# Row means of a two-layer convolution network on one core: taken from the rounded input and from sums kept in a first pass, instead of from the layer's output

## The reference

```python
def _L0_conv_ref(x, weight_int8, scale_weight, bias):
    scale_input = jnp.max(jnp.abs(x_cl)) / 2.0 ** (ACTBIT - 1)
    x_q = jnp.round(jnp.clip(x_cl / scale_input, -n, n))          # n = 127
    acc = conv3x3(x_q, w_hwio)                                    # padding 1
    out = acc * (scale_input * scale_weight) + bias
def _L1_conv_ref(x, w_real, w_imag, b_real, b_imag):
    X = jnp.fft.rfftn(x, axes=(-2, -1))
    Yr = _rconv(Xr, wr) - _rconv(Xi, wi) + b_real                 # 3x3 over frequencies
    Yi = _rconv(Xr, wi) + _rconv(Xi, wr) + b_imag
    return jnp.fft.irfftn(Y, axes=(-2, -1))

x = x + _L0_conv_ref(_gn(x), ...)
x = x + _L1_conv_ref(_gn(x), ...)
```

## Time and profile before

| | us |
|---|---|
| median of 3 runs | 3697.43 |
| lowest, highest | 3686.82, 3706.25 |
| profiled execution, its own time | 3688.6 |
| span of its trace | 3686.8 |
| mean granted TensorE clock, share of full | 0.995 |

### The profile page before, as it was taken

How to read it: one execution, slowest core, us unless ns; L and a number is a source line. 1 busy time by engine, 2 the same in 40 slices (tenths; PEclk the granted TensorE clock), 3 DMA queues, 4 the chain that set the end, 5 groups by cost and what they waited for, 6 DMA issues and landing times.

```text
span 3686.8 us, 126585 instructions
## 1 busy us (share of the span) xinstructions
PE 2952.2 (80%) x45732; PEld 2630.6 (71%) x45732; DVE 3147.2 (85%) x5880; ACT 1888.0 (51%) x2799; POOL 1481.3 (40%) x1984
## 2 busy tenths in 40 slices
PE   0000004899999999999999999999999999999998
PEld 0000002688888888888888888888888888888888
DVE  8999995688888888888888888888888888888886
ACT  8999991344444444444444444444444444444443
POOL 4777100344444444434443333443443433344444
PEclk9999999999999999999999999999999999999999
DMA  8777760366666666666666666666666666666655
GB/s 312 239 239 239 239 216 13 100 205 197 201 199 203 202 200 200 204 197 200 201 202 195 197 194 193 202 197 197 204 199 196 204 194 192 201 193 206 199 181 180
DMA packets 630696, 730.98 MB, mean 198 GB/s; under 512 B 76752, under 2 KB 602160, under 8 KB 614736
## 3 DMA queue, kind: packets, MB, share of 16 engines
q1 hardware_dynamic: 482640, 588.71, 50.1%
q10 hardware_dynamic: 147456, 134.28, 12.7%
HBM read 262.58 MB, written 134.22 MB: 108 GB/s over the span
## 4 chain that ended last, share of the span: by engine, by line
PE 54%; SPq 13%; DMA 11%; issue 11%; DVE 7%; ACTq 1%; ACT 1%; POOL 1%; DVEq 0%; POOLq 0%
PE y_ps L986 14%; PE mean_b L1031 9%; PE x_ps L973 7%; PE conv_ps L1018 7%; SPq L464 7%; PE fin_ps L1005 6%; DMA halo<-quant 4%; DMA out<-img 4%; PE t_ps L964 4%; SPq L386 3%; PE conv_ps L1020 2%; DVE scaled L763 2%; DMA img<-in_x 2%; PE fin_ps L1000 2%; DVE scaled L764 1%
## 5 line engine op out<-in xcount | busy, mean ns | idle before, releaser
L734 POOL TENSOR_SCALAR eo<-img,norm 128x256 f32<-128x256 f32 x512 | 477.9, 933 | 1458.5 <-PE t_ps L964 1248.9
L986 PEld LDWEIGHTS y_ps<-mix_w,stack 128*128 128x128 f16 x24576 | 793.5, 99 | 119.6 <-DMA stack<-xn 6.0
L986 PE MATMUL y_ps<-mix_w,stack 128*128 128x64 f16 x24576 | 809.3, 194 | 4.5 <-DMA stack<-xn 4.4
L562 ACT ACTIVATE y_hi<-y_ps 128x512 f16<-128x512 f32 x512 | 305.6, 597 | 889.3 <-PE y_ps L986 889.3
L548 ACT ACTIVATE xt<-t_ps 128x512 f32<-128x512 f32 x512 | 305.7, 597 | 629.2 <-PE t_ps L964 506.6
L973 PE MATMUL x_ps<-dft,xt 128*128 128x128 f32 x4096 | 541.6, 275 | 0.0
L839 DVE SCALAR_TENSOR_TENSOR img<-conv_ps,cst,img 128x512 f32<-128x512 f32 x512 | 383.1, 748 | 169.3 <-PE conv_ps L1020 153.1
L1031 PE MATMUL mean_b<-row_mean,img 128*128 128x48 f32 x4096 | 512.8, 273 | 8.4 <-DVE img L839 8.4
L1031 PEld LDWEIGHTS mean_b<-row_mean,img 128*128 128x128 f32 x4096 | 504.1, 196 | 18.2 <-DVE img L839 17.5
L826 DVE SCALAR_TENSOR_TENSOR xn<-x_ps,norm,xn 128x512 f16<-128x512 f32 x512 | 383.7, 750 | 140.7 <-ACT xn L555 120.0
L973 PEld LDWEIGHTS x_ps<-dft,xt 128*128 128x128 f32 x4096 | 498.3, 192 | 0.0
(11 more groups left out here) (134 smaller groups left out, 5111.6 us busy)
## 6 DMA issues: line engine op xcount, KB each, us to landing
stack<-xn SPq DMA_DIRECT2D x2048, 132.0 KB, 2.7
img<-in_x SPq DMA_DIRECT2D x1024, 128.0 KB, 2.9
out<-img ACTq DMA_DIRECT2D x1024, 128.0 KB, 3.0
img<-in_x SPq DMA_DIRECT2D x120, 1024.0 KB, 4.9
halo<-quant SPq DMA_DIRECT2D x192, 193.3 KB, 3.3
halo<-quant SPq DMA_DIRECT2D x64, 169.1 KB, 3.2
row_mean<-table_row_mean SPq DMA_DIRECT2D x1, 768.0 KB, 15.4
spread<-table_spread SPq DMA_DIRECT2D x1, 512.0 KB, 14.6
```

Source lines behind the costliest of these rows:

```text
L734: nc.gpsimd.tensor_scalar(even, rows[:, :, 0:F], norm[v][:, 2:3], None, ALU.add).then_inc(shift_s, 1)
L986: last = nc.tensor.matmul(y_ps[t % 2][:, g, b, :], stack[:, t % 2, g, first:first + F], mix_w[:, 2 * at + b, g, f, part, :], start=i == 0, ...
```

## The change

The row means of the result of layer 0 are no longer summed from that result. They are the sum of two parts. The first part are the row means of the input itself, and PE takes them in the first phase, while each image is there for its statistics; they are written to DRAM (`kept`, 128x96 float32 an image) and read back later. The second part are the row means of what layer 0 adds: the convolution commutes with the sum over rows, so the rounded input is summed over its rows first (`rounded_w`, 128 weights in float16: the three waves in two halves each, and the first and the last row) and a small product an image (`conv_a`) does the 3x3 weights after.

- First phase: PE gets `image_means`, 64 float32 products of 48 columns an image. They are of the form of the products that `row_means` did. PE waits for all tables before the first, and for ACT's copy of the image two before. SP waits for PE (`p1_pe`) too before it reloads a quarter, ACT waits for PE at the end of an image and copies the sums (`rmx`), SP stores them (`keep`).
- Main phase: `row_means` is now two float16 products of 258 columns a pair, right behind `conv_pair` of that pair, with its weights `rounded_w` and the moving `quant`. `mean_rows` at t = 12 is six small float32 products and the two that were there. ACT copies `rq_ps` at t = 9, DVE adds the two parts at t = 12 (`row_sum`), where ACT copied before. SP loads the kept sums at t = 6. DVE's rounding waits for `rq_s` (convolution and row means of the quarter) in place of `conv_s`.
- `quant`, `halo` and the layer 0 weights are float16 instead of bf16. Two tables of 768 KB and one of 1024 KB are loaded more, one of 768 KB less.

```diff
+    def image_means(i, u, tab):
+        n = 2 * i + u
+        for q in range(QU):
+            pe.wait_ge(load_s[u][q], loaded(i))
+            if q == 0:
+                pe.wait_ge(sums_s, n + 1)
+            for hb in range(QB * q, QB * q + QB):
+                for half in range(2):
+                    last = nc.tensor.matmul(sums_ps[u][half], img[u][:, hb, F * half:F * half + F], tab[:, 48 * hb:48 * hb + 48],
+                                            start=hb == 0, stop=hb == HB - 1)
+            last.then_inc(p1_pe, 1)
...
             pe.wait_ge(table_s, 16 * len(TABLES))
+            with pe.Fori(0, SP2 - 1) as i:
+                for u in range(2):
+                    image_means(i, u, sums[1])
+            for u in range(2):
+                image_means(SP2 - 1, u, sums[0])
...
+                        sp.wait_ge(p1_pe, (2 * i + u - 2) * QU + q + 1)
                         load_runs(2 * i + u + 2, u, q)
+                    keep(2 * i + u - 2, 2 * i + u, u)
...
+                act.wait_ge(p1_pe, QU * (n + 1))
+                act.wait_ge(kept_s[u], 16 * (i + 1))
+                nc.scalar.activation(rmx[:, u, 0:48], sums_ps[u][0], ACT.Copy)
+                nc.scalar.activation(rmx[:, u, 48:96], sums_ps[u][1], ACT.Copy).then_inc(sums_s, 1)
...
-            def row_means(k, u, c):
-                pe.wait_ge(x1_s, done(k, c))
-                if c == 0:
-                    pe.wait_ge(meanc_s, k + 1)
-                    nc.tensor.matmul(mean_b[:, 0:96], ident[:], zeros[:], start=True, stop=False)
-                for hb in (2 * c, 2 * c + 1):
-                    for half in range(2):
-                        nc.tensor.matmul(mean_ps[half], img[u][:, hb, F * half:F * half + F], row_mean[:, hb, :],
-                                         start=False, stop=False)
+            def row_means(k, c):
+                pe.wait_ge(quant_s, PAIRS * k + c + 1)
+                if c == 0:
+                    pe.wait_ge(rqe_s, k + 1)
+                for hb in (2 * c, 2 * c + 1):
+                    last = nc.tensor.matmul(rq_ps, rounded_w[:, hb, :], quant[:, hb, :], start=hb == 0, stop=hb == HB - 1)
+                last.then_inc(rq_s, 1)
+            def mean_rows(k, u):
+                pe.wait_ge(rqe_s, k + 2)
                 pe.wait_ge(zb_s, k + 1)
                 for half in range(2):
+                    for dw in range(3):
+                        nc.tensor.matmul(mean_ps[half], rq[:, F * half + dw:F * half + dw + F], conv_a[:, dw, :],
+                                         start=dw == 0, stop=False)
                     last = nc.tensor.matmul(mean_ps[half], norm[u][:, 2:3].to_broadcast([P, P]), channel[:],
...
-                    if conv and t == IMAGE_AT:
-                        act.wait_ge(mean_s, s + 2)
-                        nc.scalar.activation(row_t[:, 0, :], mean_ps[0], ACT.Copy)
-                        nc.scalar.activation(row_t[:, 1, :], mean_ps[1], ACT.Copy).then_inc(meanc_s, 1)
+                    if conv and t == STATS_AT - 1:
+                        act.wait_ge(rq_s, PAIRS * (s + 3))
+                        nc.scalar.activation(rq[:], rq_ps, ACT.Identity, scale=q_scale).then_inc(rqe_s, 1)
...
+            def row_sum(k, i, u):
+                dve.wait_ge(rmx_s[u], 16 * (i + 1))
+                dve.wait_ge(mean_s, k + 1)
+                nc.vector.tensor_tensor(row_t[:], misc_ps[:, 96:192].rearrange("p (a x) -> p a x", a=2),
+                                        rmx[:, u].rearrange("p (a x) -> p a x", a=2), ALU.add).then_inc(meanc_s, 1)
```

129 lines of the change are left out of this document (101 added, 28 removed).

## The result

| | before | after |
|---|---|---|
| median of 4 runs beside each other, us | 3694.26 | 3963.47 |
| lowest, highest | 3686.82, 3706.25 | 3939.27, 3968.39 |
| profiled execution, its own time | 3688.6 | 3959.38 |
| mean granted TensorE clock | 0.995 | 0.972 |

A forecast was written before the change was run, and what follows sets the result against it. The prediction took DVE's reductions to bound the first phase and PE the main phase. Its terms summed as 3688.6 + 299 - 15 - 186 = 3786.6, forecast 3787 us, 2.4% slower, range 3665 to 3880.

The forecast's parts named there:

- Part 1, the price of a product in the first phase: First phase: products stay at 1.2 GHz, 0.41 us each, 26.2 us an image, so PE becomes the bound: +299 us.
- Rival A: First phase: the clock rises, 13.4 us an image hides behind DVE, costing +15; total 3503 us; chance 0.17.
- Part 2, the ramp: First image's convolutions after the first phase: 12 steps get shorter without float32 means, -15 us, bounds -5 to -25.
- Part 3, a period of the main phase: Main phase: PE loses net 8.7 us of work an image; -6.0 a period taken, -186 us, bounds -78 to -295.
- Then what is late next: Main phase: halo waits grow, the statistics keep their latency, clock may fall; PE's 3.4 us idle a period set against it.
- the load at t = 6: Main phase: SP's 48 KB load is one issue in a queue with slack, costed at nothing.
- rival C: Main phase: PE falls to 1.2 GHz twice a period, gaining 2.6 us instead of 6.0; total 3892 us; chance 0.09.
- Rival B: Main phase: low clock holds in the first phase, but a period gains 9 us; total 3694, no change; chance 0.12.
- DVE as a floor: Main phase: DVE's 4.62 us lap is close behind PE's new 4.71 us step, so not all 8.7 us comes out.

The follow-up runs named there:

- E2: The kernel before with 64 float32 products an image added to its first phase and its old main phase kept: 4013.89 us, ratio 1.0884.
- E3: The changed kernel with the first phase's operands swapped: table columns as weights, 256 image columns moving, 32 products an image for 64: 3699.31 us, ratio 1.0025.
- E6: E1 with halo transfers for the first image only, later images reusing its rows: 3527.79 us, ratio 0.9523 to the kernel before.
- E5: E1 with the halo transfers issued ahead of `stack`'s in SP's queue, at the end of the step before: 3651.03 us, ratio 0.9847 to the kernel before.
- E10: The kernel before with E5's edit, halo transfers issued ahead of the restacking: 3699.84 us, ratio 1.0015.
- E4: E1 with SP loading the pair whose store was issued three steps ago instead of two: 3643.84 us, ratio 0.9868 to the kernel before.
- E9: E1 with image loads issued by GpSimd instead of SP, three steps behind their store: 3618.27 us, ratio 0.9785 to the kernel before.
- E8: E5 with the statistics' first product at t = 10 behind the convolution instead of in front: 3611.96 us, ratio 0.974 to the kernel before.
- E7: E1 with 16 unused float16 products ahead of the convolution at t = 1 and 5 and the statistics at t = 10: 3618.85 us, ratio 0.9753.
- E1: The changed kernel with 8 instead of 64 products an image in the first phase, leaving out seven eighths of the sums: 3657.10 us, ratio 0.991.
- E12: The changed kernel with the edits of E3, E5 and E8, plus eight filler products each at t = 5, 8, 9 and 10: 3614.86 us, ratio 0.9792.

## Why the prediction was wrong

**Part 1, the price of a product in the first phase: right in its mechanism, its size too small.** The clock stayed at 1.2 GHz through 873.8 us without a gap, and PE became the bound. The first phase cost +333.4 us where the term had +299, since a product takes 0.427 us and not 0.41. The 0.41 was read from a block in the chain, 3.28 us for sixteen records, over eight products. That is the way from the block's start to the convolution behind it; eight products at 0.427 are 3.41, so a block is 0.13 shorter than its products in a long stream, and no long stream was in the trace. It was inside the bounds given (26.2 to 28.2 us an image; it is 27.3). Of the miss of 172 us (+270.6 against +98) this is 34.

Rival A, the clock that rises, fell for these products. The Trainium skill, page "TensorE: Matmul & The Clock Gate", section "What's actually happening", says that "activity releases the throttle". Here the trace and E2 (first product at 30.56 us, (904.4 - 30.56) / 2048 = 0.427 us each) disagree for a stream that shows as fully busy. E3 shows the other half: the same sums in products with 256 moving columns rose to the high clock, 0.94 of full over the stretch from 45 us on.

**Part 2, the ramp: right.** -19.1 us against -15. The steps of 2.80 us stand in the profile after (from 937.17 to 939.97 and from 945.22 to 948.02), and so does the wait of 3.35 us for the halo that was foreseen. Some of its steps ran at the high clock already (three products of a convolution in 0.81 us at 953.13, 1.44 before), which the term did not have; whether they are the 4 us of difference isn't shown.

**Part 3, a period of the main phase: this step failed.** "I take -6.0 a period, 31 periods: -186 us" measured -1.4 a period, -43.6 us: 142 of the 172 us. Of the net of PE's own work, -8.7, 7.5 came out where the clock was as before (E6, above). What failed is the step "Then what is late next". It named the halo, the statistics and the clock, but set the idle time of before against them and priced them at nothing beyond DVE's floor, and for the load at t = 6 it took SP's queue to have slack. The halo with `stack`, the statistics and the clock took, of the 8.7,

- 2.8 us an image more of halo waits and 0.7 of `stack`. The forecast had "its transfers take the same time while steps get shorter". The 4.4 us that the halo takes to land are a part of it, but the larger part is its place in SP's queue, behind image loads and restacking (moved ahead of the restacking in E5, its waits fall from 148.0 to 27.1 us): SP's issues alone are 4.8 us a step against PE's new 4.71. E6, without the halo, gives back 4.4 us a period. E5 and E10 show that another order only exchanges the waits, E4 that the wait for the store in front of the queue was a part, E9 that some of them stay even when SP has time. The forecast could have read this before the run, from SP's 84 us of issues in 94.1.
- 1.5 us in the chain of the statistics. E8 cuts 0.8 us of a period there without touching SP.
- some 1.3 us by the clock, which falls behind these waits. E7 shows it alone: work added in the waits makes the kernel 1.0 to 1.6% faster. The forecast put this into rival C, with a chance of 0.09.

Rival C comes nearest of the cases in the period (92, measured 92.7) and in its reason, waits that lower the clock; its 3892 us lacked the waits' own length and the 34 us of the first phase. Rival B, 9 us a period, is shown wrong by the 1.4 of the changed kernel and the 0.7 of E1.

**DVE as a floor.** The forecast gave 2.7 of the 8.7 us to DVE. In the changed kernel DVE hardly shows as what PE waits for outside the statistics (5.1 us for `y_lo` in 2700). In E6 DVE is busy 2417.03 us of the stretch, but in 30.3 images: 79.7 us each, as in E1 (79.1), and PE still waits only 7.5 us for `y_lo`. In E9 DVE's own work got longer with the edit. So no run shows the term, and none rules it out: the kernel never got down to where it would count, and E6's 89.0 has 2.5 us an image of waits for `stack` in it.

**What stays open.** How much of SP's lateness is the wait for the store and how much the number of issues behind it: E4 took the first away and E9 both in part, and each moved its image loads too. Why E3's period is 0.9 longer than E1's. And why the period of E12 isn't shorter than 91.8 with the clock at 1.00: about 3 us an image of `stack` waits are left, and its filler adds some 3.5 us to PE's work, and no run took either away.

## What to carry to other kernels

Price work that is moved to an idle engine at the clock that it will get there, and choose the form of the product with that in mind: here one choice of the moving operand was worth 323 us of the first phase, and 264 us of the whole time. When steps get shorter, write down what each queue must issue in one and whether it still fits (here 84 us of issues a period of 94.1): a queue that was just in time can take most of the gain, and a transfer that is moved ahead in it delays those behind it. A wait of TensorE costs its own length and then what the clock loses.

## What the runs showed that was not expected

- Float32 products with 128x128 weights and 48 moving columns, back to back for 873.8 us and 100% busy, ran at 1.2 GHz to the last: 0.427 us each, as much as a 512-column float16 product there (0.43), and 0.21 at the high clock.
- Useless products speed a kernel up: E7, 0.9753 (0.9712 to 0.9795) against 0.991 (0.9878 to 0.9942), with the granted clock from 0.96 to 0.99.
- With the image loads issued by GpSimd one of DVE's instructions took 586 ns in place of 433 (E9).
